# Spectral mixing with one load and one split for both rows of a symmetric frequency pair, and a share of the splits on GpSimd

## What is computed

```python
    def _L0_conv_ref(X, kernel_base):
        ...
        Xf = jnp.fft.fftn(X, axes=(1, 2), norm='forward')
        ...
        r2 = f1[:, None] ** 2 + f2[None, :] ** 2
        kernel = kernel_base[r2]
        Xm = Xf[:, idx1[:, None], idx2[None, :], :]
        Ym = jnp.einsum('xyij,bxyj->bxyi', kernel, Xm)
        ...
        return jnp.fft.ifftn(Yf, s=(S1, S2), axes=(1, 2), norm='forward').real
    ...
    x = x + _L0_conv_ref(_ln_c(x), L0_conv_kernel_base)
```

## Time and profile before

| | before |
|---|---|
| median of 3 runs | 1204.75 us (1203.93 to 1208.91) |
| the profiled execution | 1205.99 us |
| its span | 1204.2 us |
| PE busy | 912.3 us (76%) |
| DVE busy | 911.8 us (76%) |
| ACT busy | 576.0 us (48%) |
| POOL busy | 660.4 us (55%) |

### The profile page before, as it was taken

How to read it: one execution, slowest core, us unless ns; L and a number is a source line. 1 busy time by engine, 2 the same in 40 slices (tenths; PEclk the granted TensorE clock), 3 DMA queues, 4 the chain that set the end, 5 groups by cost and what they waited for, 6 DMA issues and landing times.

```text
span 1204.2 us, 24945 instructions
## 1 busy us (share of the span) xinstructions
PE 912.3 (76%) x8490; PEld 699.6 (58%) x8490; DVE 911.8 (76%) x2088; ACT 576.0 (48%) x1163; POOL 660.4 (55%) x532
## 2 busy tenths in 40 slices
PE   5964469776778777887369999999247887788887
PEld 5863468663445444554269999999124454445454
DVE  6978976677977788799956777754568788777884
ACT  1336854476655565530034444442576556555500
POOL 1542000325877687778474443310437777787787
PEclk9955579977889999999879999999559998899998
DMA  9865600010899992000358778883000000000000
GB/s 387 280 280 118 165 2 1 2 43 0 325 397 398 396 397 90 1 2 1 116 169 281 266 253 277 268 268 118 1 1 18 36 19 35 17 24 29 36 32 39
DMA packets 52865, 168.18 MB, mean 140 GB/s; under 512 B 13616, under 2 KB 13872, under 8 KB 51120
## 3 DMA queue, kind: packets, MB, share of 16 engines
q1 hardware_dynamic: 52784, 167.18, 39.3%
HBM read 98.68 MB, written 68.49 MB: 139 GB/s over the span
## 4 chain that ended last, share of the span: by engine, by line
PE 40%; DVE 24%; ACT 17%; issue 9%; POOL 6%; DMA 2%; ACTq 1%; DVEq 0%; SPq 0%; POOLq 0%
PE pair L1364 19%; ACT pair L1047 10%; DVE R L784 5%; PE pair L1332 5%; PE pair L1282 3%; PE pair L1329 3%; POOL R L458 3%; DVE R L829 3%; DVE work L612 2%; PE pair L1318 2%; PE pair L1319 2%; DVE R L721 2%; PE pair L1296 2%; DVE work L603 2%; ACT X L1081 1%
## 5 line engine op out<-in xcount | busy, mean ns | idle before, releaser
L784 DVE TENSOR_TENSOR R<-pair,R 128x1024 f32<-128x1024 f32 x256 | 310.0, 1215 | 96.7 <-PE pair L1319 90.6
L458 POOL TENSOR_TENSOR R<-R 128x1024 f32<-128x1024 f32 x128 | 304.4, 2378 | 123.1 <-DVE R L784 122.0
L1364 PE MATMUL pair<-R 128*128 (+4 forms) x2880 | 227.8, 243 | 21.6 <-DVE R L836 21.6
L1364 PEld LDWEIGHTS pair<-R 128*128 128x128 f16 x2880 | 224.9, 98 | 24.7 <-issue 22.0
L1318 PE MATMUL pair<-work,R 128*128 128x512 f16 x512 | 203.3, 397 | 35.6 <-DVE R L784 35.5
L1319 PE MATMUL pair<-work,R 128*128 128x512 f16 x512 | 201.2, 393 | 0.0
L1047 ACT ACTIVATE pair<-X,work 128x64 f32 (+1 forms) x496 | 168.8, 394 | 25.2 <-DVE R L721 20.0
L468 POOL TENSOR_TENSOR R<-R 128x512 f32<-128x512 f32 x128 | 163.1, 1274 | 11.3 <-POOL R L458 2.5
L845 DVE COPY R<-R 128x1152 f32<-128x1152 f32 x64 | 91.4, 1429 | 78.9 <-PE pair L1364 78.1
L1329 PE MATMUL pair<-X,ident_sb 128*128 128x256 f32 (+1 forms) x256 | 89.6, 434 | 76.3 <-ACT X L1081 67.0
L1332 PE MATMUL pair<-R,ident_sb 128*128 128x256 f32 x512 | 145.2, 410 | 0.0
(11 more groups left out here) (131 smaller groups left out, 1408.4 us busy)
## 6 DMA issues: line engine op xcount, KB each, us to landing
taps_halves<-R SPq DMA_DIRECT2D x128, 458.5 KB, 6.4
R<-taps_halves SPq DMA_DIRECT2D x64, 917.0 KB, 4.7
R<-spec_re SPq DMA_DIRECT2D x34, 256.0 KB, 4.1
X<-x_rows SPq DMA_DIRECT2D x4, 2048.0 KB, 20.9
R<-x_chan SPq DMA_DIRECT2D x4, 2048.0 KB, 25.3
X<-x_tok SPq DMA_DIRECT2D x4, 2048.0 KB, 13.9
out<-X SPq DMA_DIRECT2D x16, 512.0 KB, 2.6
R<-taps SPq DMA_DIRECT2D x2, 603.0 KB, 7.2
```

Of the source, the lines that this page charges most:

```text
L458: pool.tensor_tensor(h, pr[:, :, 0:256], pr[:, :, 256:512], ALU.add).then_inc(half_ready, 1)
L784: dve.tensor_tensor(pr.rearrange("p (k c) -> p k c", c=C), pair[p % 2][:, :].rearrange("p (k c) -> p k c", c=C), g.unsqueeze(2).to_broadca ...
L1364: mm = pe.matmul(acc[:, y0:y1, x0:x1, :], blocks[i % 2][:, ks, 2 - y, 1 - x, :], src[:, y0 + y:y1 + y, x0 + x:x1 + x, :], start=(ks == 0 a ...
```

## The change

Rows a and 15-a now make one step t (t from 0 to 7). Its 17 matrices are (t, b) for b from t to 15 and (15-t, b) for b from 15-t to 15; the others of the two rows are taken from the symmetry: a product with the matrix of (a, b) has 32 columns, those of (a, b) and those of (b, a) (`both`), and 16 on the diagonal. 8 steps replace 16 items, each loaded in four DMAs. The results of a step are rows a right of the diagonal and columns a below it, so it is read from PSUM in up to four views (`mixed_views`), by ScalarE and by VectorE.

The last row comes first; the edge, whose matrices are those of the last row by symmetry, is no longer loaded but copied by GpSimd from `k_last`. The order of items is `MIX_ORDER`. The low parts of steps 0, 3 and 6 and of the last row are made by GpSimd, in two operations, a scaling in place and a subtraction; the rest stays with VectorE. ScalarE makes the last row's high part and step 0's between pieces 2 and 3 of the first DFT. GpSimd's memsets are cut into four. TensorE's wait for a row's low part depends on who makes it (`wait_row_low`), as does SP's wait before it loads step t+3.

```diff
--- before.py
+++ after.py
@@ -100,15 +100,14 @@
...
-        edge_raw = R3[:, N2 + 64:N2 + 64 + 2048].rearrange("p (r a o) -> p r a o", r=2, a=16)
...
-        k_raw = [R1[:, 1024 * i:1024 * (i + 1)].rearrange("p (b o) -> p b o", b=16) for i in range(3)]
-        k_row = [f16(R1, 3072 + 2048 * i, 2048).rearrange("p (s b o) -> p s b o", s=2, b=16) for i in range(3)]
-        k_edge = f16(R1, 9216, 4096).rearrange("p (s r a o) -> p s r a o", s=2, r=2, a=16)
-        k_last = f16(R1, 13312, 18 * P).rearrange("p (s b o) -> p s b o", s=2, b=18)
+        k_last = f16(R1, 0, 18 * P).rearrange("p (s b o) -> p s b o", s=2, b=18)
+        k_raw = [R1[:, 2304 + 1088 * i:2304 + 1088 * (i + 1)].rearrange("p (b o) -> p b o", b=17) for i in range(3)]
+        k_row = [f16(R1, 5568 + 2176 * i, 2176).rearrange("p (s b o) -> p s b o", s=2, b=17) for i in range(3)]
+        k_edge = f16(R1, 12096, 4096).rearrange("p (s r a o) -> p s r a o", s=2, r=2, a=16)
...
+        NROW = 8
+        POOL_ROWS = (0, 3, 6)
+        VECTOR_ROWS = (1, 2, 4, 5, 7)
+        MIX_ORDER = ("last", 0, 1, "edge", 2, 3, 4, 5, 6, 7)
+        NMIX = len(MIX_ORDER)
...
+
+        def wait_row_low(eng, t):
+
+            if t in POOL_ROWS:
+                eng.wait_ge(k_low_p, 2 * POOL_ROWS.index(t) + 2)
+            else:
+                eng.wait_ge(k_low, 2 * VECTOR_ROWS.index(t) + 2)
+
+        def mixed_views(item, s):
+
+            psum = bank[MIX_ORDER.index(item) % 4]
+            if item == "edge":
+                return [(psum[:, 0:256].rearrange("p (a g) -> p a g", a=16), z[:, s, 0:16, :, 16])]
+            if item == "last":
+                return [(psum[:, 0:NF * 16].rearrange("p (f g) -> p g f", f=NF), z[:, s, 16, :, 0:NF])]
+            views = []
+            for a, at in ((item, 0), (15 - item, 16 + 32 * (15 - item))):
+                n = 15 - a
+                if n:
+                    row = psum[:, at + 16:at + 16 + 32 * n].rearrange("p (f h g) -> p h g f", h=2, g=16)[:, 0]
+                    views.append((row, z[:, s, a, :, a + 1:16]))
+                first = psum[:, at:at + 16]
+                column = bass.AP(first.tensor, first.offset, [list(first.ap[0]), [32, n + 1], [1, 16]])
+                views.append((column, z[:, s, a:16, :, a]))
+            return views
...
-            for a in range(16):
-                if a == 0:
+            for t in range(NROW):
+                if t == 0:
                     sp.wait_ge(c_dft, 16)
-                if a >= 3:
-                    sp.wait_ge(k_low, 2 * (a - 2))
+                if t >= 3:
+                    wait_row_low(sp, t - 3)
                 for r in BLOCKS:
-                    sp.dma_start(k_raw[a % 3][r], spec_re[:, a, 0:16, :]).then_inc(k_in[a % 3], 16)
-                if a == 2:
+                    sp.dma_start(k_raw[t % 3][r, 0:16 - t], spec_re[:, t, t:16, :]).then_inc(k_in[t % 3], 16)
+                    sp.dma_start(k_raw[t % 3][r, 16 - t:17], spec_re[:, 15 - t, 15 - t:16, :]).then_inc(k_in[t % 3], 16)
+                if t == 2:
...
-                    sp.wait_ge(h_dft, 16)
-                    for r in BLOCKS:
-                        sp.dma_start(edge_raw[r, 0], spec_re[:, 0:16, 16, :]).then_inc(edge_in, 16)
-                        sp.dma_start(edge_raw[r, 1], spec_im[:, 0:16, 16, :]).then_inc(edge_in, 16)
...
                 if n == 18:
                     pool.wait_ge(c_dft, 16)
-                    pool.memset(R1[:, 3072:7168], 0.0).then_inc(zeros_ready, 1)
+                    pool.memset(R1[:, 5568:7744], 0.0).then_inc(zeros_ready, 1)
+                if n == 26:
+                    pool.wait_ge(c_dft, 24)
+                    pool.memset(R1[:, 7744:9920], 0.0).then_inc(zeros_ready, 1)
                 c_dft_low_part(n)
-            pool.memset(R1[:, 7168:13312], 0.0).then_inc(zeros_ready, 1)
+
+            def row_low(t):
+
+                raw, row = k_raw[t % 3], k_row[t % 3]
+                pool.wait_ge(k_high, 2 * t + 2)
+                pool.tensor_scalar(raw, raw, SCALE, None, ALU.mult).then_inc(k_scaled_p, 1)
+                pool.wait_ge(k_scaled_p, POOL_ROWS.index(t) + 1)
+                for i, r in enumerate(BLOCKS):
+                    pool.tensor_tensor(row[r, 1, :, r], raw[r], row[r, 0, :, r], ALU.subtract).then_inc(k_low_p, 1)
+                    pool.wait_ge(k_low_p, 2 * POOL_ROWS.index(t) + i + 1)
+
+            pool.memset(R1[:, 9920:12096], 0.0).then_inc(zeros_ready, 1)
+            row_low(0)
+            pool.wait_ge(last_high, 1)
+            pool.tensor_scalar(last_raw, last_raw, SCALE, None, ALU.mult).then_inc(last_scaled, 1)
+            pool.wait_ge(last_scaled, 1)
+            pool.tensor_tensor(k_last[:, 1], last_raw, k_last[:, 0], ALU.subtract).then_inc(last_low, 1)
+            pool.wait_ge(c_dft, 32)
+            pool.memset(R1[:, 12096:16192], 0.0).then_inc(zeros_ready, 1)
+            pool.wait_ge(last_low, 1)
+            pool.wait_ge(zeros_ready, 4)
+            lo, hi = BLOCKS
+            pool.tensor_copy(k_edge[lo, :, 0, :, lo], k_last[lo, :, 0:16, lo]).then_inc(edge_ready, 1)
+            pool.wait_ge(edge_ready, 1)
+            pool.tensor_copy(k_edge[hi, :, 0, :, hi], k_last[hi, :, 0:16, hi]).then_inc(edge_ready, 1)
+            pool.wait_ge(edge_ready, 2)
+            pool.tensor_copy(k_edge[lo, :, 1, :, lo], k_last[lo, :, 0:16, hi]).then_inc(edge_ready, 1)
+            pool.wait_ge(edge_ready, 3)
+            pool.tensor_scalar(k_edge[hi, :, 1, :, hi], k_last[hi, :, 0:16, lo], -1.0, None, ALU.mult
+                               ).then_inc(edge_ready, 1)
+            pool.wait_ge(edge_ready, 4)
+            row_low(3)
             pool.wait_ge(h_dft, 16)
             pool.memset(R3[:, N2:N2 + 32], 0.0).then_inc(room_clear, 1)
+            row_low(6)
...
-            def matrix_low(a):
-
-                if a == 16:
-                    dve.wait_ge(k_high, 2 * 16 + 1)
-                    dve.scalar_tensor_tensor(out=k_last[:, 1], in0=last_raw, scalar=SCALE, in1=k_last[:, 0],
+            def row_low(t):
+
+                raw, row = k_raw[t % 3], k_row[t % 3]
+                for i, r in enumerate(BLOCKS):
+                    dve.wait_ge(k_high, 2 * t + i + 1)
+                    dve.scalar_tensor_tensor(out=row[r, 1, :, r], in0=raw[r], scalar=SCALE, in1=row[r, 0, :, r],
                                              op0=ALU.mult, op1=ALU.subtract).then_inc(k_low, 1)
...
+                row_low(t)
+            for n, item in enumerate(MIX_ORDER):
+                dve.wait_ge(mixed_high, n + 1)
+                for (src, low_), (_, high_) in zip(mixed_views(item, 1), mixed_views(item, 0)):
+                    last = dve.scalar_tensor_tensor(out=low_, in0=src, scalar=DOWN1, in1=high_, op0=ALU.mult,
+                                                    op1=ALU.subtract)
+                last.then_inc(mixed_low, 1)
+                if item in range(NROW) and item + 3 in VECTOR_ROWS:
+                    row_low(item + 3)
...
+            def last_high_part():
+
+                act.wait_ge(last_in, 8 * 16)
+                act.mul(last_raw[64:128, 0:17, 0:64], last_raw[64:128, 0:17, 0:64], -1.0)
+                act.mul(last_raw[0:64, 17, 64:128], last_raw[0:64, 17, 64:128], -1.0).then_inc(negated, 1)
+                act.wait_ge(negated, 1)
+                act.mul(k_last[:, 0], last_raw, SCALE).then_inc(last_high, 1)
+
+            def row_high(t):
+
+                if t < 3:
+                    act.wait_ge(zeros_ready, t + 1)
+                else:
+                    act.wait_ge(mixed, MIX_ORDER.index(t - 3) + 1)
+                act.wait_ge(k_in[t % 3], 64 * (t // 3 + 1))
+                for r in BLOCKS:
+                    act.mul(k_row[t % 3][r, 0, :, r], k_raw[t % 3][r], SCALE).then_inc(k_high, 1)
...
+                    last_high_part()
+                    row_high(0)
+            row_high(1)
...
+            row_high(2)
+            for n, item in enumerate(MIX_ORDER):
+                act.wait_ge(mixed, n + 1)
+                for src, high_ in mixed_views(item, 0):
+                    last = act.mul(high_, src, DOWN1)
+                last.then_inc(mixed_high, 1)
+                if item in range(NROW) and item + 3 < NROW:
+                    row_high(item + 3)
...
+            def both(a, b):
+
+                def columns(t):
+                    one, two = xf2[:, t, a, 2 * b:2 * b + 2, :], xf2[:, t, b, 2 * a:2 * a + 2, :]
+                    return bass.AP(one.tensor, one.offset, [list(one.ap[0]), [two.offset - one.offset, 2], [1, 2 * B]])
+                return columns
...
+            for n, item in enumerate(MIX_ORDER):
+                psum = bank[n % 4]
+                if n >= 4:
+                    pe.wait_ge(mixed_low, n - 3)
+                if item == "last":
+                    pe.wait_ge(last_low, 1)
...
+                    for b in range(NF):
+                        dst = psum[:, b * 16:(b + 1) * 16]
```

(104 more changed lines are left out.)

1 line of the change is left out of this document (removed).

## The result

| | before | changed |
|---|---|---|
| median of 15 runs each | 1205.83 us | 1198.9 us |
| ratio, 95% interval | | 0.9941 (0.992 to 0.9962) |
| span of the profiled execution | 1204.2 us | 1195.8 us |
| first transpose (end of the mixing) | 164.84 us | 158.99 us |
| from there to the end of the span | 1039.4 us | 1036.8 us |

The mixing gives 5.9 of the 8.4 us between the two spans. The other 2.6 lie behind it, where nothing was changed: over the nine profiles of this study the stretch from the first transpose to the end took between 1032.9 and 1041.5 us, so a difference of that size says nothing.

A forecast was written before the change was run, and what follows sets the result against it. VectorE was taken to bound the mixing; after the change GpSimd's chain, summed from 91.4 us, ends it at 155.9 instead of 164.8, 8.9 us less, giving 1195.9 us, rounded to 1196, range 1187 to 1211.

The forecast's parts named there:

- edge copies with turns: On GpSimd before row 3: four copies of 2048 at 2.6 us and four turns of VectorE's splits, 14.6 us.
- from row 6's split to the transpose: End of the mixing: VectorE's two splits of row 7, 2.5 us, then its reads of steps 5, 6, 7 at 2.0.
- One-input operations on GpSimd: Scaling and copying in the mixing, 13,760 elements in series at 1.2 ns each; bounds 0.857 and 2.11 ns.
- rival (3): GpSimd's chain in the mixing becomes a worse bound than VectorE was, one-input operations at 2.11 ns: 1213 us; chance 0.16.
- Two-input rate: GpSimd's subtractions in the mixing: 2.11 ns an element plus 0.19 us, bound 2.54 ns.
- The port: In the mixing, GpSimd and VectorE operations with two SBUF inputs take turns; each split meeting GpSimd's chain costs 1.27 us.
- VectorE's own sum: VectorE's work in the mixing: 30.4 us from 103.0 until 133.4, so it is no longer the bound.
- Scattered writes: Column views written by PSUM reads in the mixing: 4.1 ns a scattered element, 2.0 us a step on each engine.
- Ahead of the mixing: First and second DFT: smaller memsets against ScalarE's added 5.7 us, net 0.3 us earlier (bounds 1 earlier, 1 later).
- Line rate: GpSimd's scaling and copying in the mixing run near the memset's 0.857 ns: 1191 us; chance 0.22.
- The gain eaten (2): GpSimd's one-input operations in the mixing at 1.66 ns leave 2.0 us less than today: 1203 us; chance 0.23.
- Rival (4): GpSimd's chain is short or unblocked; ScalarE's ring with scattered writes ends the mixing, some 145: 1185 us; chance 0.03.

The follow-up runs named there:

- the first experiment: GpSimd's scaling left out of the changed kernel (low parts made from unscaled matrices): first transpose 142.69 us, median 1182.95 us, ratio to before 0.981.

## Why the prediction was right, and where it wasn't

The forecast of the mechanism held: GpSimd's list sets the end of the mixing, in the order that was written, and the first experiment shows that time taken off this list comes off the mixing. The signs named in advance are there too: no gap on GpSimd from 90.6 to 134.4, TensorE's wait of 10.57 us at the edge item, 8.10 us of waiting for row 6. The size is about right: 5.9 us in the mixing against 8.9 forecast, 7.1 us in the time against 8.9. But that it is right is in good part luck: one term was wrong by nearly as much as the whole gain forecast, and others cancelled it. Term by term, forecast and trace:

| term of the sum | forecast | measured | difference |
|---|---|---|---|
| GpSimd ready | 91.4 | 90.6 | -0.8 |
| row 0 | 6.5 | 7.7 | +1.2 |
| last row | 8.0 | 11.1 | +3.1 |
| memset of the edge | 3.5 | 3.6 | +0.1 |
| edge copies with turns | 14.6 | 11.4 | -3.2 |
| row 3 | 6.5 | 8.1 | +1.6 |
| load and high part of row 6 | 8.3 | 8.3 | 0 |
| row 6 | 6.6 | 9.7 | +3.1 |
| from row 6's split to the transpose | 8.5 | 6.6 | -1.9 |

**One-input operations on GpSimd: the step that failed.** The prediction took one rate, 1.2 ns, for two kinds. The copy runs at 0.9 ns an element (1.89 us for 2048), near the memset of the earlier trace rows. `tensor_scalar` runs at 2.6 to 2.7: 2.96 us for 1088, 6.03 for 2304, 5.36 for 2048 in float16. That is dearer than a two-input operation (2.29 us for 1088). The Trainium skill, GPSIMD Engine Reference, section Engine selection, calls operations with one input roughly line rate; by this trace that holds for the copy and not for `tensor_scalar`. The mean over the 13,760 elements is 1.9 ns. That is above the 1.8 at which the prediction said that it would be wrong, and from which rival (3), GpSimd as the worse bound, was to decide; by that sign of its own it failed. Without turns at the port these operations took 26.0 us where the sum has 17.5, so this alone would have used up 8.5 of the 8.9 us of gain. The kernel is faster all the same because the two-input operations took 1.7 us less than forecast, the turns in GpSimd's list 1.1 less, GpSimd was ready 0.8 earlier, and the tail behind row 6's split was 1.9 shorter; none of this was foreseen.

**Two-input rate.** 2.11 forecast; 4.58 us for two subtractions of 1088 is 1.9 to 2.0 ns an element without the fixed part of 0.19 us. Right, on the good side, and with mixed types it is no dearer than the float32 rows; the strided rows there, at 2.54 and 2.60, were the wrong bound for it.

**The port.** Forecast: four turns on the chain in front of row 3 (4.1 us). Measured on GpSimd: 0.4 at the last row's subtraction (5.01 for the 4.57 that it takes alone), 0.5 at row 3's scaling, 2.1 at row 6's subtraction (6.66 for 4.58), and next to nothing at the copies, as VectorE's splits of row 4 stood waiting through the 5.36 us of the last one (5.64 us for two, where the earlier trace rows have 2.46). The mechanism was right, the side that pays was not: where GpSimd's operations follow without a gap, it is mostly VectorE that waits (4.71 and 5.52 us for a split of 1.28, while GpSimd lost 0.4). The sentence on VectorE's own sum, no longer the bound, held only because its waits had slack. In the experiments in which it had none, 8.1 us were lost.

**Scattered writes.** 4.1 ns for an element was right: a column view of 240 elements took VectorE 1.17 us, a row view of 224 only 0.39. The step came to 1.65 us, not 2.0: in the timeline each of the four instructions starts before the one ahead of it has ended. The -1.9 has another make-up than the sum says, though. The sum put row 7's two splits (2.5 us) and the reads of three steps (6.0) behind row 6's split, which ends at 152.4. In the trace VectorE did those splits (until 150.3) and the reads of step 5 (until 152.0) before that, the second split between GpSimd's two subtractions, which cost GpSimd the 2.1 us named above. Behind row 6's split came TensorE's steps 6 and 7 (from 152.56), ScalarE's reads (from 154.12) and VectorE's of two steps (from 155.77): a chain through three engines that the sum does not have. TensorE's 51 matmuls, 15 of 17 products with 32 columns, took 1.41 to 1.44 us a step (4.24 for three, 2.88 for two) and 1.52 where they run by themselves, as forecast.

**Ahead of the mixing.** The DFT's reads end at 102.6, 1.06 us earlier (103.6), more than the net 0.3: VectorE's wait at 61.24 is gone, its reads of the first half start 1.4 us earlier (67.78 against 69.18), and what ScalarE's 5.7 us delayed was made up.

**The rivals.** Line rate held for the copies alone. The worse bound (3) didn't come. The gain eaten (2) was the nearest: 1203 against the forecast's 1196, with 1198.9 between them, inside the band of 1193 to 1200 that stood for a rate of 1.0 to 1.45 ns; the rate was 1.9. Rival (4), 1185 us, did not occur; yet the kernel whose mixing GpSimd doesn't hold up took 1185.82 us: the pairs without GpSimd's share, with the last row first and the edge copied by ScalarE behind step 3, are worth 22.6 us of mixing (142.27), with GpSimd's share 5.9. The prediction did not price this other way, though its own terms allow it: six more splits of 1.27 and one of 2.6 put VectorE's end at 143.6 instead of 133.4, well before the 155.9 of GpSimd's chain. So it missed that GpSimd's share costs most of what the pairs give.

## What to carry to other kernels

Work moved from a bound engine to an idle one is a gain only if its length there, dearer per element and in one chain, ends before the first engine would have ended; compare the two sums, not the idle time. Price each kind of instruction on GpSimd by its own row, and give it work that lies where VectorE has no operation with two SBUF inputs: in this kernel three rows, the last row and the edge copies were not worth giving to it; the fastest version gave it one row ahead of the others, whose worth by itself was not measured. When the symmetry halves the work, undo the offload and measure again.

## What was not expected of the hardware

`tensor_scalar` on GpSimd takes 2.6 to 2.7 ns an element, in float32 and float16, where a copy takes 0.9 and a multiplication with a broadcast operand 1.75 to 1.84. And at the shared port both sides lose: beside GpSimd's four copies six splits of VectorE lost 8.1 us while the copies themselves took 2.88, 2.85, 2.83 and 6.29 us instead of 1.9 and 5.36.
